# Making the scaled adjacency of three graph stages once: a four-layer graph network kernel on one Trainium2 core

## The reference

```
loop = arange(n);  src = concat(edge_index[0], loop);  dst = concat(edge_index[1], loop)
deg = segment_sum(ones, dst);  deg_inv_sqrt = rsqrt(deg)
norm = deg_inv_sqrt[src] * deg_inv_sqrt[dst]
out = segment_sum((x @ W)[src] * norm[:, None], dst) + b
```

## Time and profile before

| | |
|---|---|
| median of 3 runs | 3457.87 us (3457.13 to 3461.19) |
| the profiled execution's own time | 3452.86 us |
| its span, first to last instruction | 3451.1 us |
| PE busy | 3123.8 us, 91% of the span |
| DVE busy | 1746.5 us, 51% |
| POOL busy | 1421.5 us, 41% |
| ACT busy | 750.5 us, 22% |
| mean granted TensorE clock | 0.937 of full speed |

### The profile page before, as it was taken

The page is one execution under the profiler, slowest core; times in us unless marked ns, Lnnn a source line. Parts: engine busy times, 40 slices in busy tenths (PEclk is TensorE's granted clock), DMA queues, the critical chain, the costliest instruction groups (busy, mean ns, idle before and its releaser), DMA issues.

```text
span 3451.1 us, 39618 instructions
## 1 busy us (share of the span) xinstructions
PE 3123.8 (91%) x14183; PEld 2459.9 (71%) x14183; DVE 1746.5 (51%) x2948; ACT 750.5 (22%) x1316; POOL 1421.5 (41%) x1007
## 2 busy tenths in 40 slices
PE   8999798999999968989766879899999998979978
PEld 3576577788888855768545568678888886768858
DVE  7634798466554355347675344543334437641131
ACT  1044111333332212112124112110111113121122
POOL 2021387344344523635300024446666654516500
PEclk9999898999999989999877779999999999989986
DMA  2011365122112211212200122223233322203213
GB/s 78 21 46 35 114 210 178 51 65 70 59 55 69 83 41 52 87 55 87 69 0 9 60 92 64 69 66 101 87 100 96 96 87 70 77 28 100 92 48 109
DMA packets 91268, 256.99 MB, mean 74 GB/s; under 512 B 10335, under 2 KB 10975, under 8 KB 90852
## 3 DMA queue, kind: packets, MB, share of 16 engines
q1 hardware_dynamic: 80352, 219.45, 20.9%
q10 hardware_dynamic: 10788, 35.83, 3.0%
HBM read 253.67 MB, written 1.57 MB: 74 GB/s over the span
## 4 chain that ended last, share of the span: by engine, by line
PE 83%; DVE 10%; issue 3%; ACT 2%; POOL 1%; DMA 0%; DVEq 0%; ACTq 0%; POOLq 0%
PE ps L413 22%; PE ps L417 21%; PE ps L418 21%; PE ps L889 2%; DVE aux L1818 2%; PE ps L515 1%; PE ps L509 1%; PE ps L1124 1%; PE ps L996 1%; PE ps L1027 1%; PE ps L768 1%; PE ps L779 1%; PE ps L761 1%; PE ps L753 1%; DVE hot L2140 1%
## 5 line engine op out<-in xcount | busy, mean ns | idle before, releaser
L361 POOL TENSOR_SCALAR w_hi<-raw 128x768 fp32r<-128x768 f32 x498 | 455.7, 915 | 1805.8 <-PE ps L413 1463.3
L364 POOL TENSOR_TENSOR w_lo<-raw,w_hi 128x768 fp32r<-128x768 f32 x498 | 974.1, 1956 | 41.5
L413 PE MATMUL ps<-H_hi,w_hi 128*128 128x512 f32 x804 | 318.9, 397 | 20.2 <-issue 15.5
L417 PE MATMUL ps<-H_lo,w_hi 128*128 128x512 f32 x804 | 316.5, 394 | 0.0
L418 PE MATMUL ps<-H_hi,w_lo 128*128 128x512 f32 x804 | 316.5, 394 | 0.0
L413 PE MATMUL ps<-B_hi,w_hi 128*128 128x512 f32 x720 | 291.7, 405 | 21.0 <-DVE B_lo L1616 14.9
L413 PE MATMUL ps<-A_hi,w_hi 128*128 128x512 f32 x780 | 307.8, 395 | 1.8 <-DVE sel_now L2062 1.8
L417 PE MATMUL ps<-A_lo,w_hi 128*128 128x512 f32 x780 | 304.7, 391 | 0.0
L418 PE MATMUL ps<-A_hi,w_lo 128*128 128x512 f32 x780 | 304.1, 390 | 0.0
L417 PE MATMUL ps<-B_lo,w_hi 128*128 128x512 f32 x720 | 283.3, 393 | 0.0
L418 PE MATMUL ps<-B_hi,w_lo 128*128 128x512 f32 x720 | 282.7, 393 | 0.0
(11 more groups left out here) (438 smaller groups left out, 5955.8 us busy)
## 6 DMA issues: line engine op xcount, KB each, us to landing
raw<-stream_dram SPq DMA_DIRECT2D x558, 384.0 KB, 3.0
w_ring<-w_dram ACTq DMA_DIRECT2D x39, 384.0 KB, 3.5
u_rows<-rows_dram ACTq DMA_DIRECT2D x8, 768.0 KB, 6.0
rows<-rows_dram ACTq DMA_DIRECT2D x7, 768.0 KB, 4.1
w_last<-w_dram ACTq DMA_DIRECT2D x9, 384.0 KB, 3.6
x<-x_dram ACTq DMA_DIRECT2D x1, 1536.0 KB, 8.9
out_dram<-x ACTq DMA_DIRECT2D x1, 1536.0 KB, 5.1
orf<-orf_dram ACTq DMA_DIRECT2D x6, 192.0 KB, 3.1
```

The lines of the kernel that those rows point to most:

```text
L361: pool.tensor_scalar(w_hi[:, b // 3, b % 3], raw[:, b // 3, b % 3], 1.0, 1.0, ALU.mult, ALU.mult)\
L364: pool.tensor_tensor(w_lo[:, b // 3, b % 3], raw[:, b // 3, b % 3], w_hi[:, b // 3, b % 3], ALU.subtract)\
L413: mm = pe.matmul(o, wh, xh, start=first, stop=False, skip_group_check=True)
L417: pe.matmul(o, wh, xl, start=False, stop=False, skip_group_check=True)
```

## The change

The scaled adjacency is made once, in ffn1, and kept as `spread` in the memory of `w1_ring`, which only layer 0 uses; the counts plus identity stand meanwhile in `counts_f` (the first `exp_02` buffer). Layers 2 and 3 only make e_hi and e_lo from it.

- In ffn1, DVE converts the counts and adds the identity before it adds the first of the six chunks to x; PE's `degrees` stands after the first of the six blocks with n = 1, in bank 0; after the sixth chunk DVE copies the degrees, and the root, the reciprocal, the four diagonal picks and the four products follow, all ahead of the last three small additions at L2348. ACT's root stands at the end of its part of ffn1.
- In gnn2 and gnn3, PE's `degrees` between the groups of `turn_n` is gone, and so is `gcn`. ACT rounds `spread` to e_hi (`spread_high`) and goes straight on to `features_n`. DVE's `spread_low` makes e_lo; in layer 3 it stands ahead of `add_t(acc)` of mix3.
- `graph_t` waits for the features in two halves: the signal for its first three output chunks comes when DVE has finished the B_lo of group 0, that for the last three after group 1.

```diff
-            def graph_t(reader):
+            def graph_t(reader, halves=False):
                 for j in range(KC):
+                    if halves and j % 3 == 0:
+                        pe.wait_ge(dve_to_pe, S.due(dve_to_pe))
                     use(j)
...
             def degrees():
                 pe.wait_ge(dve_to_pe, S.due(dve_to_pe))
-                use(6)
-                for m in range(NT):
-                    mm = pe.matmul(ps[:, 6], ones[:, :], aux[:, m], start=m == 0, stop=m == NT - 1, skip_group_check=True)
-                done(mm, 6, "dve")
+                use(0)
+                for m in range(NT):
+                    mm = pe.matmul(ps[:, 0], ones[:, :], counts_f[:, m], start=m == 0, stop=m == NT - 1, skip_group_check=True)
+                done(mm, 0, "dve")
...
                         whole_block_used()
+                        if (n, f) == (1, 0):
+                            degrees()
...
             if part("gnn2"):
-                turn_n(A, "act", lambda g, m: degrees() if (g, m) == (0, NT - 1) else None, normed)
-                pe.wait_ge(dve_to_pe, S.due(dve_to_pe))
-                graph_t("dve")
+                turn_n(A, "act", since=normed)
+                graph_t("dve", True)
...
                 mark(act_to_dve)
-
-            def gcn():
                 act.wait_ge(dve_to_act, S.due(dve_to_act))
                 act.activation(row[:, :], row[:, :], ACT.Sqrt).then_inc(act_to_dve, 1)
-                for m in range(NT):
-                    high(e_hi[:, m], scr[:, m])
-                act.wait_ge(dve_to_act, S.due(dve_to_act))
-                features_n()
+
+            def spread_high():
+                for m in range(NT):
+                    act.copy(e_hi[:, m], spread[:, m]).then_inc(act_to_dve, 1)
...
+            def degrees():
+                for m in range(NT):
+                    S.step(dve.tensor_copy(counts_f[:, m], counts[:, m]))
+                    c = slice(m * P, m * P + P)
+                    ins = dve.tensor_tensor(counts_f[:, m, c], counts_f[:, m, c], ident[:, :], ALU.add)
+                ins.then_inc(dve_to_pe, 1)
+                for j in range(KC):
+                    patches(j)
+                dve.wait_ge(tile_for["dve"], S.due(tile_for["dve"]))
+                freed(dve.tensor_copy(row[:, :], ps[:, 0]), 0)
+                mark(dve_to_act)
+                dve.wait_ge(act_to_dve, S.due(act_to_dve))
+                S.step(dve.reciprocal(row[:, :], row[:, :]))
+                for m in range(NT):
+                    S.step(dve.tensor_tensor_reduce(scr[:, 5, 0:P], ident[:, :], row[:, m * P:m * P + P], 1.0, 0.0, ALU.mult,
+                                                    ALU.add, nv[:, 14, m:m + 1]))
+                for m in range(NT):
+                    ins = dve.scalar_tensor_tensor(out=spread[:, m], in0=counts_f[:, m], scalar=nv[:, 14, m:m + 1], in1=row[:, :],
+                                                   op0=ALU.mult, op1=ALU.mult)
+                S.step(ins)
...
-            def gcn(bias):
-
-                for m in range(NT):
...
+            def spread_low():
+
                 for m in range(NT):
                     dve.wait_ge(act_to_dve, S.due(act_to_dve))
-                    dve.tensor_tensor(e_lo[:, m], scr[:, m], e_hi[:, m], ALU.subtract)
-                mark(dve_to_act)
-                features_n()
-                mark(dve_to_pe)
-                add_t(x, bias)
+                    dve.tensor_tensor(e_lo[:, m], spread[:, m], e_hi[:, m], ALU.subtract)
...
                 linear_attention("attention3", 0.0)
+                spread_low()
                 add_t(acc, "L3_mix_proj_b")
             if "gnn3" in parts:
-                gcn("L3_gnn_b")
+                features_n(marked=True)
+                add_t(x, "L3_gnn_b")
```

More of the change, by code:

```diff
@@ L271, in build @@
         hidden = exp_1[0]
+        counts_f = exp_02[0]
+        spread = w1_ring[:, :, :].rearrange("p a d -> p (a d)")[:, 0:NT * N].rearrange("p (m n) -> p m n", m=NT)
         elu_exp = exp_02[1]
@@ L1073, in _ @@
             if part("gnn3"):
-                turn_n(A, "act", lambda g, m: degrees() if (g, m) == (0, NT - 1) else None, plain)
-                pe.wait_ge(dve_to_pe, S.due(dve_to_pe))
-                graph_t("dve")
+                turn_n(A, "act", since=plain)
+                graph_t("dve", True)
             if part("mlp3"):
@@ L1531, in _ @@
             if "gnn2" in parts:
-                gcn()
+                spread_high()
+                features_n()
             if "mix2" in parts:
@@ L1723, in _, with features_n @@
             flat = aux[:, :, :].rearrange("p a n -> p (a n)")
-            def features_n():
+            def features_n(marked=False):
                 for g in range(2):
@@ L1730, in features_n @@
                         ins = dve.tensor_tensor(bn[1][:, m, c], sn[:, m, c], bn[0][:, m, c], ALU.subtract)
+                    if marked:
+                        ins.then_inc(dve_to_pe, 1)
                 return ins
@@ L1914, in add_t, with patches @@
                     freed(ins, j)
+            def degrees():
[3 more added lines that the diff above has]
+                    ins = dve.tensor_tensor(counts_f[:, m, c], counts_f[:, m, c], ident[:, :], ALU.add)
+                ins.then_inc(dve_to_pe, 1)
+                for j in range(KC):
[12 more added lines that the diff above has]
+                S.step(ins)
+            def patches(j):
+                dve.wait_ge(tile_for["dve"], S.due(tile_for["dve"]))
+                freed(dve.scalar_tensor_tensor(out=x[:, j, NCLS:N], in0=ps[:, j, NCLS:N], scalar=col("L1_ffn_fc2_b", j),
+                                               in1=x[:, j, NCLS:N], op0=ALU.add, op1=ALU.add), j)
             def gat_sum(bias):
@@ L2384, in _ @@
             if "gnn2" in parts:
-                gcn("L2_gnn_b")
+                spread_low()
+                features_n(marked=True)
+                add_t(x, "L2_gnn_b")
             if "mix2" in parts:
```

14 lines of the change are left out of this document (removed).

## The result

The changed kernel takes 3428.47 us, the median of four runs (3425.07 to 3431.64), against 3457.5 (3453.73 to 3461.19) before: a ratio of 0.9919, interval 0.9904 to 0.9933. Its profiled execution took 3425.07 us with a span of 3422.9; before it was 3452.86 and 3451.1.

A forecast was written before the change was run, and what follows sets the result against it. PE was taken to bound the kernel, with 83% of the chain. Terms -15.4 (gnn2), -15.7 (gnn3) and +3.4 (ffn1) sum to -27.7 us: 3425.2 against the profiled 3452.86, median 3430; 8-in-10 range 3422 to 3441.

The forecast's parts named there:

- gnn2 and gnn3: Graph stages of layers 2 and 3: time from degree passes to `graph_t` falls to 13.0 us, saving 15.4 and 15.7.
- the passes: PE's degree passes between the groups of `turn_n` in gnn2: removing them saves 3.4 us.
- the stop and its restart: PE's pause between the groups in gnn2, 8.7 us, and the half-clock tiles behind it, 1.6 us, both removed.
- the last wait: PE's wait just before `graph_t` in gnn2: about 1.7 us removed.
- bank 0 has time to spare: In gnn2, ACT frees bank 0 near 2052, PE wants it at 2059.1: 7 us to spare.
- ffn1, the step that was mis-sized: Added degree passes on PE in ffn1: cost 3.4 us, between -1.2 and 6.9; DVE's chain covered by 4.6 us.
- the 1.1 us: In ffn1, dense degree passes raise the clock for at least one small block behind them, giving back 1.1 us.
- the bad case: In ffn1, all four DVE picks take 1.85 us: chain 15.2 us instead of 11.8, cover 1.2 us.
- (a): Rival: DVE becomes the bound in ffn1; cost term -1.2 to +2.2, time 3425.6 to 3429.0; chance 0.07.
- the 3 us allowed: Kernel-wide: some ten shifted restarts lengthen or shorten half-level stretches, about 3 us either way, outside the sum.
- (b): Rival: waits in gnn2 and gnn3 return in part; 3433.6 with 1.7 us per layer, or 3442; chance 0.07.
- (c): Rival: without the pause PE falls to half level, group 1 through `graph_t`; 58.4 us more, 3489; chance 0.02.

The follow-up runs named there:

- e3: Changed kernel without the identity, degree passes, root, reciprocal, picks and products in ffn1, so the adjacency is the plain counts; 3424.97 us, ratio 0.9915.
- e4: Changed kernel with the degree passes moved behind the norm's sums of layer 2 and the chain of root, picks and products behind the norm; 3422.69 us, ratio 0.9905.
- e7: Changed kernel with eight dead degree passes put back between group 0 and group 1 in layers 2 and 3, without any wait; 3435.9 us (one run).
- e5: Changed kernel, but `graph_t` waits for both halves of the features before its first block; adjacency still kept; 3428.97 us (one run).
- e6: Kernel before the change with only the features marked and awaited by `graph_t` in halves, adjacency made anew in both layers; 3429.26 us (one run).
- e2: Changed kernel with picks and products moved behind the norm in layer 2, root and reciprocal staying in ffn1; 3422.53 us, ratio 0.9906.
- e1: Changed kernel with POOL's splits of layer 2's first turn held until DVE's products are finished; 3427.47 us, ratio 0.9917.
- e9: Same kernel as e6 (the kernel before with the halves alone), timed again in rounds; 3429.74 us, ratio 0.9914.
- e10: Changed kernel with two dead 128x512 matmuls between the first and second expert passes of layer 3's feed-forward stage; 3411.38 us, ratio 0.9866.
- e12: Kernel before the change with only two dead matmuls between the first and second expert passes of layer 3's feed-forward stage; 3441.84 us, ratio 0.9954.

## Why the prediction was right, point by point

**gnn2 and gnn3.** -15.4 and -15.7 were said. gnn3 measures -15.67. gnn2 measures -16.7: 15.4 as worked out, and 1.3 because group 0 ran at half level for 3 us instead of 6, which the sum had named as what it doesn't hold. e3 and e4, whose ffn1 is as short as before, keep the 6 us and save the 15.4. Two pieces have their own experiment: the passes 3.4 and 3.5 (e7), the last wait 1.7 and 1.7 (e5). What is left, 10.3 and 10.5, fits the stop and its restart, 8.7 and 1.6; no run puts them back into the changed kernel, but the stop stands whole where the chain stays (e6). That bank 0 has time to spare is borne out: ACT waits for PE, and even e2's and e4's longer chains raise no stop. One term was missed without harm: B_lo took 1.6 us a tile beside POOL, not the 0.56 of the kernel before. `spread_low` in mix3 costs nothing: DVE still idles 3.56 us ahead of `add_t(acc)`.

**ffn1, the step that was mis-sized.** +3.4 was said, between -1.2 and +6.9; it measures +5.9. PE's part is small: its last small pass ends 41.9 us behind the mark instead of 40.9, +1.0, because the degree passes cost 5.2 us (window clock 0.54 over 3.5 us of them) and four small blocks behind them give back 4.3. The Trainium skill, "TensorE: Matmul & The Clock Gate", Part 1, has activity release the gate. For the degree passes this trace and e3 agree (1.40 and 1.50 us for twelve small passes behind them, 2.61 without them), and more came back than the 1.1 us read from that rule. For the small passes they don't: PE was busy in all 2.50 us of the window of 0.53, which the prediction took as agreeing, so there the measurement decides. So PE ended 1.0 us later and not 3.4, and DVE ended last, which the text had only for small passes at full clock, with 15.2 us at most. It took 16.9 us (2004.13 to 2021.01). The picks took 5.1 us, less than the bad case, but the products 6.83 where 2.74 was carried over from gnn2, in which POOL had finished its splits by then. That is rival (a)'s mechanism with a larger price: +5.9 instead of at most +2.2. Of the 3.7 us between them the chain is 1.7, and 1.8 are the degree passes, 5.2 where (a) took 3.4. The mis-sized term is the duration taken from a place with another neighbour: e1 measures the products at 2.74 us and the picks at 0.29 without POOL, and there PE ends last again and the stage is 0.9 above the kernel before.

The Trainium skill, "SBUF — State Buffer", section "Who interferes with whom", says that a DVE instruction with two SBUF inputs contends with a GpSimd instruction that reads SBUF, and calls the contention an exclusive lock. The trace agrees that they contend: both sides stretch where they meet, the products to 1.7 us each, POOL's subtraction from 1.81 to 2.11 and its copy from 0.83 to 1.26. The long pick looks like such a lock too: it began at 2009.53, 0.10 us behind POOL's subtraction, and ended at 2011.38, 0.14 us behind its end, where 0.29 us do without POOL.

**The rest.** -1.9 us behind gnn3 and +0.5 in the norm are the clock's, inside the 3 us allowed: in the norm its sums run at half level for longer, and behind gnn3 the second expert passes give 2.5 (43.2 us instead of 45.7) and the other stretches take 0.6 back. The text had every idle stretch followed by half level; the wait of 1.6 us ahead of `graph_t` was not (window clock 1.00 behind it in the kernel before). Terms against measured: -27.7 said, -28.2 found, the ffn1 miss of 2.5 made good by the 1.3 and 1.9 that the sum had left out with either sign. That the total came within 0.5 us is luck; the two large terms are not.

**The other rivals.** (b) named 1.7 us a layer for the last wait; e5 has that very price, the changed kernel does without it. (c) is refuted: the clock is 1.00 from 2046.5 to 2070 and in `graph_t`. But a fall to half level while PE is busy, which (c) feared, does occur elsewhere: in the changed kernel's second expert passes, for some 40 us.

## What to carry to other kernels

A wait between an early and a late engine was worth its stop, the restart behind it and the passes that fed it; read from one trace, these came out within 0.3 us. A duration holds only with its neighbours: before you move a DVE operation with two SBUF inputs, look what POOL does at the new place. Compare kernels by stretches between marks that both have, since a change elsewhere can move a distant stage's clock by more than the change is worth; e6's total alone would have credited the graph stages with 22 us that came from the clock of another stage.

## What the hardware did that I had not expected

The 192 passes of 64 columns, the same code behind the same stop of 0.55 us, went three ways: at 1.00 throughout (25.2 us in e6 and e9), at 0.50 throughout (45.7 us in the kernel before), and at 1.00 for two blocks and then, with PE busy, at 0.50 (window of 39.6 us) (the changed kernel). The 192 ahead of them ran at 1.00 in all of these (24.8 us). Two dead matmuls, 2.2 us, in place of the stop were worth 17.3 us in e10, and 17.6 in e12.

In e3, 8-column passes right behind the large ones went from 1.50 to 2.61 us a block within two blocks, with PE busy throughout; behind eight passes of 512 columns in the changed kernel it was three blocks (1.40, 1.50, 1.50) before 2.13.

Four DVE products beside POOL's splits took 6.83 us instead of 2.74, while POOL's operations in the same stretch lost 0.3 to 0.4 us each.
